# Six of a scan's products and a norm's scaling on GpSimd, from SBUF

## The reference

```
x_in, res = split(x @ in_proj.T)                    # 512 channels each
u   = silu(causal_conv4(x_in) + conv_b)
dt_in, B, C = split(u @ x_proj.T)                   # 64, 16, 16
dt  = softplus(dt_in @ dt_proj.T + dt_b)
for each state n of 16, channel d, position t:
    h[t] = exp(dt[t] * A[d, n]) * h[t-1] + (dt[t] * u[t]) * B[n, t]
    y[t] += h[t] * C[n, t]
y = (y + u * D) * silu(res)
x = layernorm(x + y @ out_proj.T)                   # (z - mean) * rstd
```

## Time and profile before

| | us |
|---|---|
| median of 3 runs | 3372.53 |
| lowest, highest | 3368.55, 3373.21 |
| the profiled execution | 3369.65 |
| its span, first to last instruction | 3367.9 |
| PE busy in the span | 3023.6 (90%) |
| VectorE (DVE) busy | 2653.4 (79%) |
| ScalarE (ACT) busy | 2226.0 (66%) |
| GpSimd (POOL) busy | 2217.1 (66%) |

### The profile page before, as it was taken

How to read it: one execution, slowest core, us unless ns; L and a number is a source line. 1 busy time by engine, 2 the same in 40 slices (tenths; PEclk the granted TensorE clock), 3 DMA queues, 4 the chain that set the end, 5 groups by cost and what they waited for, 6 DMA issues and landing times. The chain is left out here.

```text
span 3367.9 us, 39358 instructions
## 1 busy us (share of the span) xinstructions
PE 3023.6 (90%) x11504; PEld 1717.0 (51%) x11504; DVE 2653.4 (79%) x3525; ACT 2226.0 (66%) x3402; POOL 2217.1 (66%) x1611
## 2 busy tenths in 40 slices
PE   3589999999999999999889999999977799999997
PEld 1157666667666667776334433443433344444443
DVE  5989999898989898554799999999997545555543
ACT  2457676767767666665566566566653688888887
POOL 3578888888888888775467776776774244444444
PEclk7689999999999999999999999999988899999999
DMA  3034444444444444554122222222222122222222
GB/s 97 13 95 133 125 129 128 119 136 121 127 129 126 127 119 130 145 146 125 58 72 71 71 72 70 72 71 70 71 72 66 63 99 99 105 105 105 106 105 94
DMA packets 199617, 335.38 MB, mean 100 GB/s; under 512 B 21379, under 2 KB 57380, under 8 KB 199020
## 3 DMA queue, kind: packets, MB, share of 16 engines
q1 hardware_dynamic: 199404, 332.86, 32.5%
HBM read 325.69 MB, written 7.09 MB: 99 GB/s over the span
## 5 line engine op out<-in xcount | busy, mean ns | idle before, releaser
L1366 POOL TENSOR_TENSOR c_hc<-c_h,c_c_rep 128x1024 f32<-128x1024 f32 x256 | 604.3, 2361 | 284.7 <-DVE c_h L1405 228.9
L1405 DVE TENSOR_TENSOR_SCAN c_h<-c_decay,c_carry,c_v_ps 128x512 f32<-128x512 f32 x512 | 632.7, 1275 | 0.5 <-DVE c_v_ps L1395 0.5
L1882 POOL TENSOR_TENSOR d_acc<-d_acc,d_prod 128x512 f32<-128x512 f32 x240 | 310.6, 1309 | 448.8 <-DVE d_prod L1950 448.7
L1287 ACT ACTIVATE c_decay<-c_dt,c_a_cols 128x512 f32<-128x512 f32 x512 | 364.3, 720 | 356.5 <-DVE c_h L1405 355.1
L1840 ACT ACTIVATE d_hmid<-d_up,d_b 128x1024 f32<-128x1024 f32 x512 | 532.0, 1118 | 76.1 <-PE d_up L1735 75.9
L1154 PE MATMUL c_y_ps<-c_hc,ident 128*128 128x512 f32 x1024 | 504.7, 617 | 44.7 <-POOL c_hc L1366 29.9
L687 POOL TENSOR_TENSOR ab_inner_low<-ab_inner,ab_inner_high 128x512 fp32r<-128x512 f32 x264 | 341.8, 1295 | 241.2 <-ACT ab_inner_high L570 239.9
L559 ACT ACTIVATE ab_gate_ps<-ab_gate_ps,ab_raw_d 128x512 f32<-128x512 f32 x264 | 174.6, 661 | 431.0 <-PE ab_gate_ps L414 430.8
L669 POOL TENSOR_TENSOR ab_hc<-ab_h,ab_c_rep 128x512 f32<-128x512 f32 x256 | 331.5, 1295 | 86.8 <-DVE ab_h L740 65.1
L1950 DVE SCALAR_TENSOR_TENSOR d_prod<-d_ring,d_b,d_w_rep 128x512 f32<-128x512 f32 x240 | 180.1, 751 | 245.0 <-PE d_ring L1745 192.6
L1735 PE MATMUL d_up<-d_heads,d_w 128*128 128x512 f32 x1024 | 328.5, 438 | 19.7 <-ACT d_hmid L1840 19.7
(11 more groups left out here) (228 smaller groups left out, 6305.1 us busy)
## 6 DMA issues: line engine op xcount, KB each, us to landing
ab_raw_gu<-in_b_experts SPq DMA_DIRECT2D x264, 256.0 KB, 3.4
ab_w_rep<-ab_w_scratch SPq DMA_DIRECT2D x264, 256.0 KB, 3.6
c_c_rep<-c_c_scratch SPq DMA_DIRECT2D x256, 256.0 KB, 3.1
d_w_rep<-d_w_scratch SPq DMA_DIRECT2D x256, 256.0 KB
ab_raw_d<-in_b_experts SPq DMA_DIRECT2D x264, 129.0 KB, 2.1
ab_raw_x<-in_xT SPq DMA_DIRECT2D x32, 256.0 KB, 4.8
out<-xT SPq DMA_DIRECT2D x8, 512.0 KB, 5.8
xT<-in_xT SPq DMA_DIRECT2D x1, 3072.0 KB, 12.6
```

The source lines that it names most:

```text
L1287: nc.scalar.activation(decay[:, i % DEC, :], dt[:, s, m, :], ACT.Exp, scale=a_cols[:, n * NM + m:n * NM + m + 1]).then_inc(decay_ready, 1)
L1366: nc.gpsimd.tensor_tensor(hc[:, q % HC], h[:, q % HR], c_rep[:, q % BC].unsqueeze(1).broadcast_to([P, PAIR, CH]), ALU.mult).then_inc(hc_re ...
L1405: nc.vector.tensor_tensor_scan(out=h[:, q % HR, m, :], data0=decay[:, i % DEC, :], data1=v_ps[m][:], initial=carry[:, i:i + 1], op0=ALU.mu ...
L1882: nc.gpsimd.tensor_tensor(acc[:, s, g, :], acc[:, s, g, :], prod[:, q % PR, :], ALU.add).then_inc(add_ready, 1)
```

## The change

In units 5, 10, 15 and 21, 26, 31 of each chunk (states 5, 10 and 15 of both pairs, `OWN`), the product with B is made by GpSimd: one 128x1024 instruction from dtu and a copy of B's row on all partitions, `b_rep`, into `v_own`, both in SBUF. TensorE makes no B matmul and VectorE no product for these units; their scans read `v_own` in place of `v_ps`. The own product of unit q + 4 stands on GpSimd behind hc of unit q, so behind q = 1, 6, 11, 17, 22 and 27. `b_rep` has three buffers, one for each state, filled by a DMA each from the DRAM scratch, which now holds B beside C, in q = 29 to 31 of the chunk before. The gates move from q = 4 and 6 to 3 and 8, `weigh_input` of the second pair from 9 to 13. dtu has one buffer instead of two. The scaling of the norm goes from VectorE at q = 30 to GpSimd behind hc of unit 31, as one 128x1024 instruction, and the inverse deviation that it reads goes to an SBUF tile, `rstd`, instead of `bank_b`.

```diff
+    OWN_N = (5, 10, 15)
+    OWN = [pair * N_STATE + n for pair in range(PAIRS) for n in OWN_N]
+    SPREAD = [q for q in range(NU) if q not in OWN]
+    LEAD = 4
-        dtu = sb("dtu", [P, 2, NM, CH])
+        dtu = sb("dtu", [P, NM, CH])
+        b_rep = sb("b_rep", [P, len(OWN_N), CH])
+        v_own = sb("v_own", [P, PAIR, CH])
+        rstd = sb("rstd", [P, CH])
@@ SyncE
-                sp.dma_start(c_dram[s], x_dbl[RANK + N_STATE:RANK + 2 * N_STATE, :]).then_inc(c_stored, 16)
+                sp.dma_start(c_dram[s], x_dbl[RANK:RANK + 2 * N_STATE, :]).then_inc(c_stored, 16)
+            def spread_own(c, s, j):
+                sp.wait_ge(c_stored, c * 16 + 16)
+                if not is_int(c, 0):
+                    sp.wait_ge(own_ready, (c - 1) * len(OWN) + len(OWN_N) + j + 1)
+                sp.dma_start(b_rep[:, j], c_dram[s, 0, OWN_N[j]:OWN_N[j] + 1, :].broadcast_to([P, CH])
+                             ).then_inc(b_loaded[j], 16)
@@ TensorE
-            spread_b(c, s, q + 1)
+            if q + 1 in SPREAD:
+                spread_b(c, s, q + 1)
@@ ScalarE, deviation
-                nc.scalar.activation(bank_b[:], bank_b[:], ACT.Exp, scale=-0.5).then_inc(rstd_ready, 1)
+                act.wait_ge(scaled, c + 1)
+                nc.scalar.activation(rstd[:], bank_b[:], ACT.Exp, scale=-0.5).then_inc(rstd_ready, 1)
@@ GpSimd
+            def own_product(c, s, q):
+                pair, at = q // N_STATE, OWN.index(q)
+                pool.wait_ge(b_loaded[at % len(OWN_N)], c * 16 + 16)
+                pool.wait_ge(dtu_ready, c * PAIRS + pair + 1)
+                if at > 0:
+                    pool.wait_ge(h_ready, c * NT + (OWN[at - 1] + 1) * PAIR + DEC)
+                elif not is_int(c, 0):
+                    pool.wait_ge(h_ready, (c - 1) * NT + (OWN[-1] + 1) * PAIR + DEC)
+                nc.gpsimd.tensor_tensor(v_own[:], dtu[:, pair_of(pair)],
+                                        b_rep[:, at % len(OWN_N)].unsqueeze(1).broadcast_to([P, PAIR, CH]),
+                                        ALU.mult).then_inc(own_ready, 1)
+            def scale(c):
+                pool.wait_ge(rstd_ready, c * 2 + 4)
+                pool.wait_ge(zc_ready, c * 2 + 4)
+                nc.gpsimd.tensor_tensor(xT[:, :, bass.ts(c % NCH, CH)], zc[:],
+                                        rstd[:].unsqueeze(1).broadcast_to([P, 2, CH]), ALU.mult).then_inc(scaled, 1)
-                    if q in (4, 6) and not first:
-                        apply_gate(c - 1, t, (q - 4) // 2)
-                    if q == 9:
+                    if q + LEAD in OWN:
+                        own_product(c, s, q + LEAD)
+                    if q in (3, 8) and not first:
+                        apply_gate(c - 1, t, (3, 8).index(q))
+                    if q == 13:
                         weigh_input(c, s, 1)
+                    if q == 31:
+                        scale(c - 1)
@@ VectorE
             def scan(c, q, m):
                 i = q * PAIR + m
-                dve.wait_ge(v_ready, c * NT + i + 1)
+                if q in OWN:
+                    v = v_own[:, m, :]
+                    dve.wait_ge(own_ready, c * len(OWN) + OWN.index(q) + 1)
+                else:
+                    v = v_ps[m][:]
+                    dve.wait_ge(v_ready, (c * NS + SPREAD.index(q)) * PAIR + m + 1)
...
-                                             data1=v_ps[m][:], initial=carry[:, i:i + 1],
+                                             data1=v, initial=carry[:, i:i + 1],
-            def scale(c):
...
-                    product(c, s, q)
+                    if q in SPREAD:
+                        product(c, s, q)
-                    if q == 30:
-                        scale(c - 1)
```

More of the change, by code:

```diff
@@ L935, in layer1_scan @@
     BLO = P - 2 * N_STATE
+    OWN_N = (5, 10, 15)
+    OWN = [pair * N_STATE + n for pair in range(PAIRS) for n in OWN_N]
+    SPREAD = [q for q in range(NU) if q not in OWN]
+    NS = len(SPREAD)
+    LEAD = 4
     F32R = mybir.dt.float32r
@@ L947, in layer1_scan @@
         bank_a, bank_b = [ctx.enter_context(nc.psum_tensor(f"c_work_{i}", [P, CH], F32)) for i in "ab"]
-        c_dram = nc.dram_tensor("c_c_scratch", (2, N_STATE, CH), F32, kind="Internal").ap()
+        c_dram = nc.dram_tensor("c_bc_scratch", (2, 2, N_STATE, CH), F32, kind="Internal").ap()
         in_w, x_w, dt_w, out_w, conv_w, vecs, a_cols, loaded = weights.all
@@ L984, in layer1_scan @@
         c_loaded = [sem(f"c_loaded{i}") for i in range(BC)]
+        b_loaded = [sem(f"b_loaded{i}") for i in range(len(OWN_N))]
+        own_ready = sem("own_ready")
         b_ready = sem("b_ready")
@@ L1024, in spread @@
                 n = q % N_STATE
-                sp.dma_start(c_rep[:, q % BC], c_dram[s, n:n + 1, :].broadcast_to([P, CH])
+                sp.dma_start(c_rep[:, q % BC], c_dram[s, 1, n:n + 1, :].broadcast_to([P, CH])
                              ).then_inc(c_loaded[q % BC], 16)
@@ L1030, in chunk @@
                     spread(c, s, q)
+                    if first and q < len(OWN_N):
+                        spread_own(0, 0, q)
                     if q == 23 and not last:
                         store_c(c + 1, 1 - s)
+                    if q - NU + len(OWN_N) >= 0 and not last:
+                        spread_own(c + 1, 1 - s, q - NU + len(OWN_N))
             store_c(0, 0)
@@ L1046, in project_x @@
                     if not is_int(r, 0, 1):
-                        pe.wait_ge(scaled, (r - 1) * 2)
+                        pe.wait_ge(rstd_ready, (r - 1) * 2)
                 else:
@@ L1142, in spread_b @@
                     pe.wait_ge(b_low, c + 1)
-                if not (is_int(c, 0) and q < BR):
-                    pe.wait_ge(v_ready, c * NT + (q - BR + 1) * PAIR)
-                nc.tensor.matmul(b_ps[q % BR][:], sel_b[:, q % N_STATE, :], b_parts[:, s, :],
+                at = c * NS + SPREAD.index(q)
+                if at >= BR:
+                    pe.wait_ge(v_ready, (at - BR + 1) * PAIR)
+                nc.tensor.matmul(b_ps[at % BR][:], sel_b[:, q % N_STATE, :], b_parts[:, s, :],
                                  start=True, stop=True).then_inc(b_ready, 1)
@@ L1184, in chunk @@
                         if last:
-                            pe.wait_ge(scaled, c * 2)
+                            pe.wait_ge(rstd_ready, c * 2)
                         mean(c - 1)
@@ L1351, in weigh_input @@
                 pool.wait_ge(u_ready, r + 1)
-                nc.gpsimd.tensor_tensor(dtu[:, s, ms], dt[:, s, ms], u[:, s, ms], ALU.mult).then_inc(dtu_ready, 1)
+                if not is_int(r, 0):
+                    spread_before = sum(q < (pair + 1) * N_STATE for q in SPREAD)
+                    pool.wait_ge(v_ready, ((r - 1) * NS + spread_before) * PAIR)
+                nc.gpsimd.tensor_tensor(dtu[:, ms], dt[:, s, ms], u[:, s, ms], ALU.mult).then_inc(dtu_ready, 1)
             def apply_gate(c, s, pair):
@@ L1391, in product @@
                     dve.wait_ge(dtu_ready, c * PAIRS + pair + 1)
-                dve.wait_ge(b_ready, c * NU + q + 1)
+                at = c * NS + SPREAD.index(q)
+                dve.wait_ge(b_ready, at + 1)
+                before = c * NU + q - 1 if q == 0 or q - 1 in SPREAD else c * NU + q - 2
                 for m in range(PAIR):
-                    dve.wait_ge(h_ready, c * NT + q * PAIR + m + 1 + DEC - PAIR)
-                    nc.vector.tensor_tensor(v_ps[m][:], dtu[:, s, pair * PAIR + m, :], b_ps[q % BR][:],
+                    dve.wait_ge(h_ready, before * PAIR + m + 1 + DEC)
+                    nc.vector.tensor_tensor(v_ps[m][:], dtu[:, pair * PAIR + m, :], b_ps[at % BR][:],
                                             ALU.mult).then_inc(v_ready, 1)
@@ L1412, in first_input @@
                 dve.wait_ge(u_ready, 1)
-                nc.vector.tensor_tensor(dtu[:, 0, ms], dt[:, 0, ms], u[:, 0, ms], ALU.mult).then_inc(dtu_ready, 1)
+                nc.vector.tensor_tensor(dtu[:, ms], dt[:, 0, ms], u[:, 0, ms], ALU.mult).then_inc(dtu_ready, 1)
             def skip(c, s, pair):
@@ L1433, in centre @@
                 if c >= 0:
-                    dve.wait_ge(scaled, (c + 1) * 2)
+                    dve.wait_ge(scaled, c + 1)
                 for half in range(2):
```

## The result

The changed kernel takes 3435.13 us (median of 4 runs, 3433.12 to 3437.04), against 3372.87 before (also of 4; one run more than in the table of times): ratio 1.0186, 95% interval 1.0169 to 1.0204, 62 us slower, 1.9%. The profiled execution took 3434.56, 64.9 more than the profiled one before. The forecast was +70, so 3442.5.

What follows compares the result with a forecast made beforehand. VectorE was taken to bound the scan stage. 136.1 us lost in own units less 66.1 gained gave +70.0: 3439.7 profiled, 3442.5 for the median of the runs; range 3392 to 3476.

Steps and rivals of the forecast that it cites:

- Taken from VectorE, 66.1: Second layer's scan: six units' products (7.08 us) and scale (1.18) leave VectorE, 8.26 per chunk, 66.1 over eight chunks.
- GpSimd's added work fits; the broadcasts of B, the single dtu and the exp into SBUF cost nothing: Scan stage: GpSimd's extra 16.5 us per chunk, 103 of 119 or more, fits; these other edits cost nothing.
- A scan with two SBUF inputs and GpSimd take turns: Own units: such a scan and a GpSimd instruction exclude each other for their whole length; 136.1 us lost; forecast 82%.
- scans of 1275 ns that are not locked out (3316): Rival, own units: scans untouched by GpSimd, units cost 2.36 us, TensorE becomes tight; 3316.5 us; 8%.
- a GpSimd that gives way between its two rows of 512 (3355): Rival, own units: GpSimd yields halfway through a 1024 instruction, units near 3.4 us; 3355 us; 5%.
- GpSimd's queued instruction first (3510): Rival, own units: GpSimd's next instruction precedes a waiting VectorE, 29 of 48 units pay another 2.36 us; 3510; 5%.
- Which own units meet a running instruction: Units 5, 10, 15, 31 begin with GpSimd busy for 1.40 us more; 21 and 26 find it idle.
- Size of an own unit: An own unit costs 5.78 us if GpSimd is at work at its start, 4.52 if idle, against 3.54 before.
- Chunk 0: First chunk of the scan: without gates and residual, own units lose 15.5 us, against 17.4 in chunks 1 to 6.
- Tail at nothing: Stage's end: scale and first gate follow hc 31 on GpSimd, ending 2587.1, before the last skip's 2587.6; no cost.

Runs made afterwards that it cites:

- Experiment 1: Kernel before with only the norm's scaling moved to GpSimd (gates, weigh_input and single dtu as in the change): 3364.31 us, ratio 0.9975.
- experiment 3: Changed kernel with own units' scans reading v_ps in PSUM, GpSimd's products made but unused: 3323.17 us, ratio 0.9853 against the kernel before.
- experiment 2: Kernel before with VectorE's products of the six own units written to SBUF and read there, no work added to GpSimd: 3459.16 us, ratio 1.026.

## Why the prediction was right, step by step

- *Taken from VectorE, 66.1.* Right. Experiment 1 gives 1.21 per chunk for scale; in experiment 3 the own units that wait for nobody cost 2.34 instead of 3.54, 1.20 each.
- *GpSimd's added work fits; the broadcasts of B, the single dtu and the exp into SBUF cost nothing.* Right: experiment 3 has them all, and its chunks are 112.86 apart.
- *A scan with two SBUF inputs and GpSimd take turns.* Right, in all its parts: who waits, that hc goes between A and B, and that a waiting VectorE comes before GpSimd's queued instruction (in unit 5 scan A ran before hc, due 0.2 into the unit). The evidence was tensor_tensor of the last layer; it held for the scan, and for GpSimd's 1024-element instructions as a whole. That ends the three rivals: scans of 1275 ns that are not locked out (3316), a GpSimd that gives way between its two rows of 512 (3355), GpSimd's queued instruction first (3510).
- *Which own units meet a running instruction.* Right: 5, 10, 15 and 31, not 21 and 26, in each chunk as listed. The rest r of the running instruction was 1.34 to 1.37 (once 1.64, the unit of 5.87), not 1.40.
- *Size of an own unit.* A little high: 5.78 and 4.52 worked out, 5.58 and 4.41 measured. A GpSimd instruction that waited ends 2.15 after the scan (2.21 taken), a scan that waited 1.08 after GpSimd (1.13 taken). How much a waiting instruction saves had been read from rows of 512 elements. Over 29 and 19 units that is 29 x 0.20 + 19 x 0.11 = 7.9 us: +62.1 instead of +70.
- *Chunk 0.* Missed: in it VectorE ran at TensorE's 3.67 per unit from unit 4 to 12 before, not at its own 3.54. Longer own units gave TensorE the time to get ahead: units 6 to 12 run at 3.54 between them, 1.0 us less.
- *Tail at nothing.* Nearly: the last skip ended 5.8 us after hc 31 began, not 7.6 as before, so the second gate waited 1.1 for scale and the first gate; from hc 31 to the first residual 12.4 us, 12.1 before.
- *Not part of the prediction.* The profiled execution began its first scan 3.0 us later than the one before (1629.41 against 1626.39). Of the seven experiments' profiles six began it at 1624.5 to 1626.8 and one at 1630.6: all but experiment 2's have the change's code before the scan. So it varies between executions, and I don't put it down to the change.

With 0.3 for the one unit of 5.87 and 0.3 for the tail: 62.1 - 1.0 + 0.3 + 0.3 + 3.0 = 64.7, of the 64.9 between the profiled executions; without the 3.0 it is 61.7, beside the medians' 62.3.

## What to carry to other kernels

Before an input or an output moves to SBUF so that GpSimd can help, count the inputs that the VectorE instruction which reads it has in SBUF. With two of them, in every row read here, a scan or a tensor_tensor ran in turn with GpSimd's tensor_tensor from SBUF, and an own unit cost 4.41 or 5.58 us where the old unit, product and all, cost 3.54. Keep one of the two in PSUM: ScalarE could write it there, and 62 us lost became 46 gained. And read lengths by form against their minimum; the wait is inside the instruction, so idle times and busy shares don't show it.

## What was not expected of the hardware

Taking turns is exact to some 20 ns: 18 of the 19 own units that met an idle GpSimd cost 4.40 to 4.42 us. The same tile read from SBUF instead of PSUM, with no other change, cost 87 us of 3373 (experiment 2), though neither engine had more to do. In the change the turns cost even more, 62 + 66 = 128 us; 66 of them are hidden, since that much was taken off VectorE.
